# Top-one expert layer over eight experts: all experts for all tokens, or tokens sorted by expert into 15 tiles

## The reference

```
h2 = rmsnorm(x, ln2_w)
logits = h2 @ Wr + br                       # 8 experts
top1 = jnp.argmax(logits, axis=-1).reshape(-1)
u = jnp.einsum('td,edf->tef', xt, W1) + b1  # W1: 8 x 128 x 512
u1, u2 = (u[..., :HID], u[..., HID:])       # HID = 256
act = u1 * jax.nn.sigmoid(u2)
y_all = jnp.einsum('teh,ehd->ted', act, W2) + b2
y = jnp.take_along_axis(y_all, top1[:, None, None], axis=1)[:, 0, :]
return x + y
```

## Time and profile before

| | |
|---|---|
| Median of 3 runs | 1660.23 us (1659.08 to 1662.02) |
| The profiled execution's own time | 1659.78 us |
| Its span, first to last instruction | 1657.9 us |
| Mean granted TensorE clock | 0.933 of full speed |
| PE busy | 1369.8 us (83%) |
| DVE busy | 1255.7 us (76%) |
| ACT busy | 897.2 us (54%) |
| POOL busy | 678.3 us (41%) |
| DMA | 42.99 MB, mean 26 GB/s |

### The profile page before, as it was taken

How to read it: one execution, slowest core, us unless ns; L and a number is a source line. 1 busy time by engine, 2 the same in 40 slices (tenths; PEclk the granted TensorE clock), 3 DMA queues, 4 the chain that set the end, 5 groups by cost and what they waited for, 6 DMA issues and landing times. The chain is left out here.

```text
span 1657.9 us, 19830 instructions
## 1 busy us (share of the span) xinstructions
PE 1369.8 (83%) x6709; PEld 729.4 (44%) x6763; DVE 1255.7 (76%) x2833; ACT 897.2 (54%) x1424; POOL 678.3 (41%) x466
## 2 busy tenths in 40 slices
PE   6677699999997757889899988989875459999798
PEld 2223344333344434355555555555564323333465
DVE  5999567866515669999999999999878657776433
ACT  4666211457543320687778778877852146666311
POOL 2656111112101034688787878878861120000012
PEclk9799899999997878999999999999987759999899
DMA  6000011000005832000000000000040300000000
GB/s 152 1 0 1 28 58 49 0 1 0 1 0 125 174 103 63 1 1 1 1 1 1 1 1 1 1 1 1 7 152 1 89 1 1 1 1 1 1 0 14
DMA packets 32482, 42.99 MB, mean 26 GB/s; under 512 B 14286, under 2 KB 25644, under 8 KB 30992
## 3 DMA queue, kind: packets, MB, share of 16 engines
q1 hardware_dynamic: 29820, 29.61, 6.2%
q10 hardware_dynamic: 2552, 12.02, 3.5%
HBM read 33.48 MB, written 8.14 MB: 25 GB/s over the span
## 5 line engine op out<-in xcount | busy, mean ns | idle before, releaser
L1631 PE MATMUL psum<-film_ka,film_context_qa 97*128 97x427 bf16 (+3 forms) x896 | 329.8, 368 | 74.3 <-DVE film_stage_kept L1810 29.4
L2033 ACT ACTIVATE film_stage_e<-psum,film_stage_bias 128x512 f32<-128x512 f32 (+1 forms) x416 | 273.9, 668 | 96.9 <-PE psum L1633 87.0
L1810 DVE MAX8 film_stage_kept<-psum 128x8 f32<-128x213 f32 (+1 forms) x960 | 318.5, 377 | 6.6 <-PE psum L1633 6.3
L1633 PE MATMUL psum<-film_kb,film_context_qb 128*128 128x427 bf16 (+2 forms) x843 | 306.4, 364 | 0.0
L1882 POOL TENSOR_TENSOR film_stage_e<-film_stage_e 128x1024 f32<-128x1024 f32 (+1 forms) x91 | 207.1, 2276 | 80.7 <-DVE film_stage_e L1852 60.8
L1852 DVE SCALAR_TENSOR_TENSOR film_stage_e<-psum,film_context_top,film_stage_e 128x512 f32<-128x512 f32 (+1 forms) x325 | 231.8, 719 | 8.4 <-ACT film_stage_e L2033 6.7
L1631 PEld LDWEIGHTS psum<-film_ka,film_context_qa 97*128 97x128 bf16 x896 | 92.1, 103 | 195.3 <-DVE film_stage_kept L1810 86.8
L3235 POOL TENSOR_TENSOR residual<-residual,top_expert_kept 128x1024 f32<-128x1024 f32 x7 | 16.5, 2351 | 294.9 <-DVE top_expert_kept L3192 294.9
L1913 PEld LDWEIGHTS psum<-ctx_rows,film_stage_mean_T 128*128 128x128 f32 (+1 forms) x816 | 121.9, 192 | 30.0 <-issue 3.3
L2998 DVE TENSOR_REDUCE gqa_attend_low<-psum 128x1 f32<-128x128 f32 (+7 forms) x128 | 94.1, 755 | 43.1 <-PE psum L2917 40.7
L1913 PE MATMUL psum<-ctx_rows,film_stage_mean_T 128*128 128x96 f32 (+1 forms) x816 | 119.9, 269 | 1.8
(11 more groups left out here) (548 smaller groups left out, 2540.3 us busy)
## 6 DMA issues: line engine op xcount, KB each, us to landing
film_kb<-film_k_rows ACTq DMA_DIRECT2D x4, 1601.0 KB
film_ka<-film_k_rows ACTq DMA_DIRECT2D x3, 1601.0 KB
ctx_T<-in_ctx_T SPq DMA_DIRECT2D x1, 2401.5 KB
gqa_experts_w<-in_L_ffn_W SPq DMA_DIRECT2D x1, 2048.0 KB
film_stage_e<-in_dft_ahead SPq DMA_DIRECT2D x1, 1728.0 KB, 8.7
film_k_rows<-cross_attention_film_hi SPq DMA_DIRECT2D x6, 256.0 KB, 2.0
film_k_rows<-cross_attention_film_mid SPq DMA_DIRECT2D x6, 256.0 KB, 2.0
film_k_rows<-cross_attention_film_low SPq DMA_DIRECT2D x6, 256.0 KB, 2.0
```

The source lines that it names most:

```text
L1631: pe.matmul(out, a["qa"][0:ROWS, h, rows], a["ka"][0:ROWS, h, c + b:c + b + cols], start=True, stop=False)
L1633: last = pe.matmul(out, a["qb"][:, h, rows], a["kb"][:, h, c + b:c + b + cols], start=False, stop=True)
L1810: last = dve.max(kept[:, h % 2, PER_PIECE * u + s, :], bank[:, lo:hi])
L2033: act.activation(e[:, n % RING, sub, 0:PIECES[u][1]], ps[:, SEARCH_BANKS + q % WEIGH_BANKS, 0:PIECES[u][1]], ACT.Exp, bias=bias[:, i % 2, ...
```

## The change

The changed kernel computes for each token only the expert that it chose. It sorts the tokens by expert into slots of a DRAM buffer, `slots`, of `NTE = NT + NE - 1 = 15` tiles of 128 rows. Each tile belongs to one expert, and 15 is the largest number of tiles that 1024 tokens of eight experts can need. All 15 are computed, filled or not.

- **Prefetch.** The loads of `W1`, `W2` and the two biases are gone from `gqa_project`. In their place stand a load of a small table, `plan`, and one store that fills `slots` with zeros.
- **Routing.** All 8 routing products, the choice, a count of tokens by expert and tile (one product with a strictly triangular matrix, eight with ones), and nine DVE operations that give each token its slot number `place_u`. Three more give each tile's expert, `owner`.
- **Scatter.** POOL issues eight indirect DMAs, each writing 128 rows of `h` (512 bytes each) into `slots` at their slot numbers.
- **Weights.** SP reads each tile's expert number into a register and loads that expert's weights and biases from one packed array, 900 numbers in each partition (450 KB in all), 15 times.
- **Tiles.** ACT issues three loads that bring the slots back (2, 4 and 9 tiles). For each tile PE transposes the rows, ACT copies them, PE computes four blocks of 128 units, ACT takes two sigmoids, DVE multiplies twice, PE adds the bias and the two halves of the second layer, DVE copies the result.
- **Results.** SP stores each tile's result to DRAM, `slot_results`. When all 15 have landed, POOL issues eight indirect DMAs that fetch, for each token tile, its rows by the same slot numbers. DVE adds each to the residual, and SP stores the output in two halves.
- The first residual add moves from DVE to POOL.

The diff, cut to what the steps need:

```diff
-N_PREFETCH = 11 + HQ
+N_PREFETCH = 9 + HQ
+NTE = NT + NE - 1
...
-                             (wt["w1"][:], t["L1_ffn_W1"].rearrange("e p n -> p e n")),
-                             (wt["w2"][:], t["L1_ffn_W2"].rearrange("e (q p) d -> p e q d", p=P)),
-                             (wt["b2"][:], t["L1_ffn_b2"])):
+                             (a["plan"][:], t["dispatch_plan"])):
...
+            sp.wait_ge(a["zeroed"], 2)
+            sp.dma_start(g["slots"].rearrange("(k p) c -> p k c", p=P),
+                         a["blank"][:].unsqueeze(1).to_broadcast([P, NTE, D])).then_inc(a["prefetched"], 16)
...
+    GROUPS = ((0, 2), (2, 6), (6, NTE))
...
-            link(dve.tensor_tensor(g["x"][:], g["x"][:], x1[:], ALU.add))
...
+            dve.tensor_tensor(own[:, 0:NT], rank[:], spread(best[:]), ALU.is_equal).then_inc(own_ready, 1)
+            dve.wait_ge(counted, 1)
+            before = ps[:, COUNT_BANK, 0:NT * NE].rearrange("p (i e) -> p i e", e=NE)
+            number = ps[:, COUNT_BANK, NT * NE:(NT + 1) * NE]
...
+            link(dve.reduce_sum(place_f[:], place[:], AX))
+            dve.tensor_copy(place_u[:], place_f[:]).then_inc(place_ready, 1)
...
+            dve.tensor_copy(owner[:], owner_f[:]).then_inc(owner_ready, 1)
+            def finish(k):
+                dve.wait_ge(y_done, k + 1)
+                dve.tensor_copy(result[:, k, :], second_out(k)).then_inc(result_ready, 1)
+            for k in range(NTE):
                 for q in range(2):
+                    dve.wait_ge(value_done, k + 1)
+                    dve.wait_ge(sig_ready, 2 * k + q + 1)
+                    dve.scalar_tensor_tensor(out=act_T[:, k, q, :], in0=value_out(k, q), scalar=weights[:, k, B1_AT + q:B1_AT + q + 1],
+                                             in1=sig[:, k, q, :], op0=ALU.add, op1=ALU.mult).then_inc(act_ready, 1)
+                if k >= 1:
+                    finish(k - 1)
+            finish(NTE - 1)
+            dve.wait_ge(rest_ready, 1)
+            for i in range(NT):
+                dve.wait_ge(row_fetched[i], 16)
+                dve.tensor_tensor(g["x"][:, i, :], g["x"][:, i, :], fetched[:, i, :], ALU.add).then_inc(added, 1)
...
+            sp.wait_ge(owner_ready, 1)
+            for k in range(NTE):
+                expert = sp.value_load(owner[0:1, k:k + 1], min_val=0, max_val=NE - 1)
+                sp.dma_start(weights[:, k, :], t["L1_expert_w"][bass.ds(expert, 1)].rearrange("o p n -> p (o n)")
+                             ).then_inc(weights_read[k], 16)
+            for k in range(NTE):
+                sp.wait_ge(result_ready, k + 1)
+                sp.dma_start(g["slot_results"][k * P:(k + 1) * P, :], result[:, k, :]).then_inc(stored, 16)
...
-                pool.tensor_tensor(g["x"][:], g["x"][:], kept[:, e % 2], ALU.add).then_inc(added, 1)
+            pool.tensor_tensor(g["x"][:], g["x"][:], x1[:], ALU.add).then_inc(rest_ready, 1)
+            pool.wait_ge(h_ready, NT)
+            pool.wait_ge(place_ready, 1)
+            for i in range(NT):
+                pool.indirect_dma_start(g["slots"], bass.IndirectOffsetOnAxis(ap=place_u[:, i:i + 1], axis=0),
+                                        h[:, i, :], None).then_inc(scattered, 16)
+            pool.wait_ge(stored, 16 * NTE)
+            for i in range(NT):
+                pool.indirect_dma_start(fetched[:, i, :], None, g["slot_results"],
+                                        bass.IndirectOffsetOnAxis(ap=place_u[:, i:i + 1], axis=0)
+                                        ).then_inc(row_fetched[i], 16)
...
+            act.wait_ge(scattered, 16 * NT)
+            for n, (lo, hi) in enumerate(GROUPS):
+                act.dma_start(slot_rows[:, lo:hi, :],
+                              g["slots"][lo * P:hi * P, :].rearrange("(k p) c -> p k c", p=P)
+                              ).then_inc(group_read[n], 16)
...
+            pe.wait_ge(own_ready, 1)
+            pe.matmul(ps[:, COUNT_BANK, 0:(NT + 1) * NE], plan["before"], own[:].rearrange("p i e -> p (i e)"),
+                      start=True, stop=False)
+            for i in range(NT):
+                last = pe.matmul(ps[:, COUNT_BANK, (i + 1) * NE:(NT + 1) * NE], ones[:],
+                                 own[:, i:i + 1, :].to_broadcast([P, NT - i, NE]), start=False, stop=i == NT - 1)
...
+            turn(0)
+            turn(1)
+            for k in range(NTE):
+                first_layer(k)
+                if k + 2 < NTE:
+                    turn(k + 2)
+                if k >= 1:
+                    second_layer(k - 1)
+            second_layer(NTE - 1)
```

More of the change, by code:

```diff
@@ L3125, in top_expert @@
+    fetched = m.sb("fetched", [P, NT, D])
+    hT = m.sb("hT", [P, S])
+    ones = m.sb("ones", [P, P])
     best = m.sb("best", [P, NT])
[L3126 to L3134, removed]
@@ L3137, in top_expert @@
[L3137 to L3146, removed]
+    rank, logits = m.sb("rank", [P, NT, NE]), m.sb("logits", [P, NT, NE])
@@ new lines, in top_expert @@
+    own = m.sb("own", [P, NT + 1, NE])
+    more, upto_tiles = m.sb("more", [P, NE, NT]), m.sb("upto_tiles", [P, NE, NE])
+    tiles, ends, starts = m.sb("tiles", [P, NE]), m.sb("ends", [P, NE]), m.sb("starts", [P, NE])
+    place, place_f, place_u = m.sb("place", [P, NT, NE]), m.sb("place_f", [P, NT]), m.sb("place_u", [P, NT], U32)
+    past, owner_f = m.sb("past", [P, NTE, NE - 1]), m.sb("owner_f", [P, NTE])
+    owner = m.sb("owner", [P, NTE], I32)
+    warm = m.sb("warm", [P, 1])
+    slot_T, sig, act_T = m.sb("slot_T", [P, NTE, P]), m.sb("sig", [P, NTE, 2, P]), m.sb("act_T", [P, NTE, 2, P])
@@ L3212, in _ @@
[L3212 to L3220, removed]
+            dve.wait_ge(logit_done, 1)
@@ new lines, in _ @@
+            link(dve.reduce_sum(tiles[:], more[:], AX))
+            link(dve.tensor_tensor(upto_tiles[:], tiles[:].unsqueeze(1).to_broadcast([P, NE, NE]), upto, ALU.mult))
+            link(dve.reduce_sum(ends[:], upto_tiles[:], AX))
+            link(dve.tensor_tensor(starts[:], ends[:], tiles[:], ALU.subtract))
+            link(dve.scalar_tensor_tensor(out=place[:], in0=starts[:].unsqueeze(1).to_broadcast([P, NT, NE]),
+                                          scalar=float(P), in1=before, op0=ALU.mult, op1=ALU.add))
@@ L3260, in _ @@
             transpose_tiles(pe, h, g["ident"][:], ps, h_ready, hT_psum)
[L3261 to L3271, removed]
-                last.then_inc(oT_psum, 1)
@@ new lines, in first_layer @@
+            def first_layer(k):
+                pe.wait_ge(turned, k + 1)
+                pe.wait_ge(weights_read[k], 16)
+                if k >= 2:
+                    pe.wait_ge(sig_ready, 2 * (k - 1))
+                    pe.wait_ge(act_ready, 2 * (k - 1))
+                for out, first, done in ((gate_out, 2, gate_done), (value_out, 0, value_done)):
+                    for q in range(2):
+                        unit = first + q
+                        last = pe.matmul(out(k, q), weights[:, k, W1_AT + unit * P:W1_AT + (unit + 1) * P], slot_T[:, k, :],
+                                         start=True, stop=True)
+                    last.then_inc(done, 1)
@@ new lines, in second_layer @@
+            def second_layer(k):
+                if k >= 2:
+                    pe.wait_ge(result_ready, k - 1)
+                pe.matmul(second_out(k), g["ones"][0:1, 0:P], weights[0:1, k, B2_AT:B2_AT + D],
+                          start=True, stop=False)
+                for q in range(2):
+                    pe.wait_ge(act_ready, 2 * k + q + 1)
+                    last = pe.matmul(second_out(k), act_T[:, k, q, :],
+                                     weights[:, k, W2_AT + q * D:W2_AT + (q + 1) * D], start=False, stop=q == 1)
+                last.then_inc(y_done, 1)
```

188 lines of the change are left out of this document (89 added, 99 removed).

## The result

The changed kernel takes 1652.45 us in the median of six runs, beside 1659.62 us for the kernel before; the ratio is 0.9944 (95% interval 0.9922 to 0.9965). One run of the six stood at 6109.74 us and is left out of the ratio; the other five lie between 1645.49 and 1654.14 us. Why that one run was so long is not known. So the change makes the kernel faster, by 7.2 us of these medians (8.1 with the long run left out, 9.3 by the ratio), where 23.2 us were forecast. In the first set of experiments the same kernel came out 12.5 us under the kernel before. The forecast of 1637.0 us had the sign, and its range of 1621 to 1658 us holds the result, but less than half of the gain came.

What follows compares the result with a forecast made beforehand. The prediction took PE to bound the part after `hT`, by sheer number of columns. Steps 1 to 11 from 1559.21 us summed to a span end of 1634.7 us, 23.2 us below before: median 1637.0 us, range 1621 to 1658 us.

Steps and rivals of the forecast that it cites:

- Steps 1 to 4: From `hT` to `place_u`: routing 3.4 us, choice 1.5, counting 3.8, slot numbers 2.3, handovers 0.2.
- Step 5: Scatter on POOL: eight indirect DMAs at 1.3 us each, 10.4 us, the last landing 2.3 us later.
- Steps 5 and 6: Scatter landing 2.3 us, then ACT's first slot load 2.3 plus 0.7 us for weights on the same DMA engines.
- step 8: SP's weight loads: some 1.2 us each, all 15 through by about 1592 us, hidden behind the tiles.
- B: Rival: issuing indirect DMAs occupies POOL over 2.75 us each; at 3.5 us, 35 us added, 1672 us; chance 0.14.
- Step 7: PE's tiles: two at 3.4 us at half clock, 13 at 1.7 us, 28.9 us in all.
- C: Rival: the clock stays at half in the tiles, thirteen losing 1.7 us each, 1659 us; chance 0.06.
- Steps 9 to 11: Last result stored 2.3 us; eight fetches at 1.3 us plus 2.3 landing; add 0.3 us, then 2.8 to span's end.
- A: Rival: row DMAs wait out their round trip one by one, 2.3 us each, not 1.3: 1653 us; chance 0.11.
- D: Rival: SP's weight loads set the pace; at 3.1 us each the end moves 6 us, 1643 us; chance 0.05.
- The upstream cost of nothing: What replaces the 3 MB prefetch, under attention, costs nothing; about 3 us if that cover were gone.

Runs made afterwards that it cites:

- the run with the clock held up: The changed kernel with 26 extra, unread PE products ahead of the tiles: 1645.09 us, ratio 0.9905.
- the repeated profile: The changed kernel executed and profiled again, unedited: 1647.89 us, ratio 0.9923.
- the 1629.4 us version: The changed kernel with weights from the fifth set on held until the first slot load landed, and the second-layer bias added on DVE: 1629.4 us, ratio 0.9806.
- the kernel with full-row products: The changed kernel with its one-row bias product made with 128 rows of 1/128 and all 128 bias rows: 1640.85 us, ratio 0.9881.
- the run with 22 products: The changed kernel with 22 extra, unread PE products of 512 columns ahead of the tiles: 1648.61 us, ratio 0.9927.

## Why the forecast was right and wrong

**Steps 1 to 4 held.** Routing took 3.60 us (forecast 3.4), counting 3.99 (3.8), the slot numbers 2.2 (2.3): 11.5 for 11.2 in all. PE at half clock after DVE's choice was the right reading of the earlier trace rows.

**Step 5, the price of an indirect DMA, held:** 1.26 us, where the middle of 0.43 and 2.35 had given 1.3. The scatters began 0.9 us after `place_u`, for which the sum had nothing. The Trainium skill's about 1 us to the first byte (DMA: Bandwidth & Descriptors, Specifications) is no measure of this spacing; by it the 16 would have been some 4 us cheaper than they are.

**Steps 5 and 6 failed in the landing.** "Plus 0.7 us because the weights use the same DMA engines": that term, which rested on no row, was at least 7.8 us in truth (22.3 less the 14.5 with eleven of fifteen sets held back). 4.9 and 7.2 us stood where 2.3 and 3.0 were forecast, and with the weights held back they were 1.3 and 2.2. The forecast had the number in hand, 6.9 MB at 397 GB/s, 17 us of full DMA engines, but asked only whether the weights came in time for the tiles. They did (step 8 held: SP issued them 1.15 us apart and PE never waited for them), at the cost of the rows that were needed first. The rival that named this traffic, B, looked for it in POOL's queue; it was in the landing, and POOL's spacing stayed 1.26 us even at a DMA share of 0.78. The same page of the Trainium skill says, under Issuing engines are not separate DMA queues, that DMAs of all engines run on the same 16 DMA engines and interleave. The runs agree, with 7.8 us.

**Step 7 failed in the price of a product and of the clock.** "Three of the second at 0.22 each" took a one-row product for one of 128 rows. No row of the kernel before had this shape; what could be read was that it was new. The nearest, eight products of 8 rows one behind the other (L3277, 1.98 us at full clock), would have given 0.25 each. Among products of 128 rows the one-row product takes 0.42 us instead of 0.22, and the work on either side of it another 0.1 us each: 2.06 us a tile where 1.7 was forecast, 5.4 us over 15 tiles. Whether the one row or the change of shape costs this was not tried. "Two tiles go at 3.4" was 12.3 us at half clock; the run with the clock held up puts that at 5.5 us, where the forecast had 3.4, so 2.1 more. Together 7.5 us, and 7.4 were missed. By the repeated profile (8.6 us at half clock) the clock took 3.8 us, so only the price of the product is missed in every execution. C, the half clock throughout, did not come, though it lasted a third of the stretch.

**Steps 9 to 11** were each a little dear: the results were stored within 1.8 us instead of 2.3, and the eighth fetch ended 11.2 us after the first began instead of 12.7. A fell: the fetches do not wait for one another (1.26 us apart, each landing after 2.4 us). D and B fell too.

**The upstream cost of nothing** for the new prefetches stands: from `gqa_project` to the last stage it was 248.2 us before and 248.8 in the mean of nine profiles since, which lie 3.8 us apart.

What stays: 10.1 us of scatter and 11.8 us of fetch in the 1629.4 us version. Storing each result row straight to its token while later tiles still run might take most of the fetch off the path; it was not tried.

## What to carry to other kernels

A transfer on the critical path must be priced against all that is queued on the DMA engines in the same time, not by its own bytes; a prefetch that has 10 us in hand should be held back until the late, small load has landed. A product with a new shape has no price in the old profile: bound it as carefully as a new DMA, or give it a shape that has one. And where PE starts from idle, take more than one profile before putting a number to the time at half clock: here the same kernel gave 8.6 and 12.3 us.

## What had not been expected of the hardware

- A product with one row (1x128) among products of 128 rows holds PE 0.42 us at full clock and leaves 0.17 us empty ahead of its weight load; one of 128 rows and the same columns takes 0.22 us, with no gap.
- With one-row products in each tile the granted clock stayed at its lower level (1.2 GHz) for 8.6 to 16.0 us of steady work in four profiles, before it rose to the higher (2.4 GHz); with none it stayed there for 5.3 and 5.5 us in two. In the kernel with full-row products it rose after 2.9 us, before the first of them. With the clock already high, one-row products did not lower it. Whether they delay the rise is not shown.
- Eight indirect DMAs of 128 rows of 512 bytes leave POOL 1.26 us apart, for writing at a DMA share of 0.78 as for reading, where the DMA engines were nearly free (0.27).
- In the run with 22 products PE's clock was full when they ended; after a pause of 3.7 us, PE's next products already ran at the half clock (0.50 from 1597.6 us on).
